# Four-layer graph network, layer 3: a wait for landed gathers in front of every second gather group

## What is computed

```python
def step(xk, _):
    msg = norm[:, None] * xk[src]
    agg = jax.ops.segment_sum(msg, dst, num_segments=n_nodes)
    return ((1.0 - ALPHA) * agg + ALPHA * h, None)
xK, _ = jax.lax.scan(step, x, None, length=10)
out = jax.nn.relu(xK)
```

## Time and profile before

| | us |
|---|---|
| median of the runs | 4953.56 |
| lowest and highest run | 4930.44, 4966.02 |
| span of the profiled execution | 6157.9 |
| of it layers 0, 1, 2 with what lies between | 3450 |
| of it layer 3, from its first gather | 2708 |

### The profile page before, as it was taken

How to read it: one execution, slowest core, us unless ns; L and a number is a source line. 1 busy time by engine, 2 the same in 40 slices (tenths; PEclk the granted TensorE clock), 3 DMA queues, 4 the chain that set the end, 5 groups by cost and what they waited for, 6 DMA issues and landing times.

```text
span 6157.9 us, 72323 instructions
## 1 busy us (share of the span) xinstructions
PE 4502.8 (73%) x25760; PEld 2814.8 (46%) x25760; DVE 2553.7 (41%) x8838; ACT 1022.9 (17%) x2922; POOL 3237.6 (53%) x3390
## 2 busy tenths in 40 slices
PE   3778477888775445446555788988888898888888
PEld 2556355566554334344444343434443444444344
DVE  6778444445443445555567422222222222222222
ACT  4656311111111000001222200000000000000001
POOL 3232365566555555555553365565656556565655
PEclk8888688899887666667767999989999999999999
DMA  5222222122222222222221555555555555555554
GB/s 136 77 83 79 77 56 52 51 58 59 55 55 57 67 70 75 68 68 69 65 71 42 160 173 159 171 158 164 172 167 164 166 178 166 161 174 161 165 170 135
DMA packets 455501, 686.46 MB, mean 111 GB/s; under 512 B 91793, under 2 KB 237879, under 8 KB 455120
## 3 DMA queue, kind: packets, MB, share of 16 engines
q1 hardware_dynamic: 341188, 454.71, 23.5%
q0 software_dynamic: 107584, 223.83, 14.0%
q10 hardware_dynamic: 6364, 3.20, 0.2%
HBM read 599.50 MB, written 82.31 MB: 111 GB/s over the span
## 4 chain that ended last, share of the span: by engine, by line
PE 42%; another core or an unknown queue 24%; DVE 18%; issue 11%; ACT 3%; DMA 1%; ACTq 0%; SPq 0%; DVEq 0%; POOL 0%; POOLq 0%
PE ps L2007 27%; PE ps L1751 5%; DVE E L2458 4%; DVE B L2538 2%; PE pt L2102 2%; DVE arena L2580 1%; PE ps L1828 1%; PE ps L2093 1%; PE pt L2038 1%; PE ps L2022 1%; DVE O L3023 1%; PE pt L1719 1%; ACT E L1561 1%; DVE scores L3019 1%
## 5 line engine op out<-in xcount | busy, mean ns | idle before, releaser
L2007 PE MATMUL ps<-arena,E 128*128 128x512 fp8e4 (+1 forms) x4900 | 1147.0, 385 | 93.6 <-issue 84.8
L2007 PE MATMUL ps<-arena,A 128*128 128x512 fp8e4 (+1 forms) x4900 | 1142.1, 385 | 62.4 <-issue 60.1
L1052 POOL DMA_INDIRECT arena<-table,src_i x810 | 776.9, 959 | 685.7 <-DMA table<-E 255.0
L1017 POOL DMA_INDIRECT E<-gat_table,src_i x782 | 759.3, 971 | 634.6 <-DVE arena L2580 367.7
L1052 POOL DMA_INDIRECT arena<-x_spill,src_i x810 | 775.3, 957 | 579.0 <-issue 225.8
L1002 POOL DMA_INDIRECT arena<-table,src_i x782 | 742.8, 950 | 583.5 <-issue 217.1
L1751 PE MATMUL ps<-E,arena 128*128 128x352 f32 (+22 forms) x2932 | 783.6, 421 | 241.1 <-DVE E L2458 155.4
L2007 PEld LDWEIGHTS ps<-arena,E 128*128 128x128 f16 x4900 | 471.4, 100 | 648.6 <-issue 193.9
L2007 PEld LDWEIGHTS ps<-arena,A 128*128 128x128 f16 x4900 | 472.9, 100 | 608.9 <-issue 154.8
L1751 PEld LDWEIGHTS ps<-E,arena 128*128 128x128 f32 x2932 | 515.4, 211 | 441.4 <-issue 195.5
L2909 DVE SCALAR_TENSOR_TENSOR C<-ps,sc_b,scores 128x128 f32<-128x128 f32 x490 | 138.9, 345 | 1295.1 <-PE ps L2022 769.3
(11 more groups left out here) (350 smaller groups left out, 4557.6 us busy)
## 6 DMA issues: line engine op xcount, KB each, us to landing
arena<-adj SPq DMA_DIRECT2D x180, 1024.0 KB
arena<-adj SPq DMA_DIRECT2D x90, 1088.0 KB
adj<-E SPq DMA_DIRECT2D x39, 784.0 KB
arena<-table,src_i POOLq DMA_INDIRECT x1592
O<-dst_rows SPq DMA_DIRECT2D x112, 224.0 KB
arena<-adj SPq DMA_DIRECT2D x20, 768.0 KB
x_spill<-A SPq DMA_DIRECT2D x55, 256.0 KB
arena<-x_spill,src_i POOLq DMA_INDIRECT x810
```

The source lines that it names most:

```text
L1017: pool.indirect_dma_start(out=att_rows[:, b % 3 * AB + at, :], out_offset=None, in_=gat_table, in_offset=bass.IndirectOffsetOnAxis(ap=src_ ...
L1052: pool.indirect_dma_start(out=y_rows[:, g % ERING, k, :], out_offset=None, in_=(table, x_spill)[half], in_offset=bass.IndirectOffsetOnAxis ...
L2007: mm = pe.matmul(chunk_banks[n % 2][:, 0:len(some) * P], y[:, i, h * D:(h + 1) * D], adj_ring[:, piece % ADJ_RING, 0:len(some), at:at + P] ...
```

## The change

In front of the gathers of groups g = 2, 4, ... 40 of each step, twenty times a step, GpSimd also waits on the `y_in` semaphore of group g - 1, the last group that it has issued, until all that group's gathers have landed. The ring, the plan and all other engines' instructions are as before.

```diff
                             for g in range(EGROUPS):
                                 pool.wait_ge(sem("edge_used"), pairs * (2 * EGROUPS) + (half * EGROUPS + g + 1))
                                 settle(pool)
+                                if g and g % 2 == 0:
+                                    r = (g - 1) % ERING
+                                    pool.wait_ge(y_in[r], (2 * pairs + half) * row_loads[r] + y_in_before[r]
+                                                 + 16 * sum(group_size(q) for q in range(r, g, ERING)))
                                 for k in range(group_size(g)):
                                     tile = edge_first + g * EG + k
                                     pool.indirect_dma_start(
```

## The result

| | us |
|---|---|
| before, median of 4 runs | 4959.79 |
| after, median of 4 runs (5393.62 to 5413.01) | 5409.67 |
| ratio, 95% interval | 1.0906 (1.0865 to 1.0947) |
| profiled execution of after, span | 5411.0 |
| profiled execution of before, seen ahead of the prediction | 6157.9 |

The forecast was 5170 with a range of 4935 to 5310. The sign came out as told, and so did the mechanism (waits of GpSimd that TensorE has to wait out). The loss is 450 us where 215 were forecast, outside the range, and also above the 375 us of the forecast's own outermost bound.

The account below looks back on a forecast made before the run. TensorE bounds layer 3 at 230 us a step; with the waits GpSimd's loop becomes 202.5 + 38 + 1.8 + 9.2 = 251.5, exposing 21.5 a step, 215 in ten: 4953.6 + 215 = 5169, rounded to 5170 us, range 4935 to 5310.

Parts of the forecast that it names:

- What bounds the kernel: Layer 3: TensorE sets the pace at 230 us a step; GpSimd is hidden with some 16 us to spare.
- The account of the median: Whole kernel: 4953.6 us can't hold both layer 3 at 2708 us and gathers of 1.25 us in layers 1 and 2.
- TensorE's own step: Layer 3: 220 us of matmuls and turns plus 9.3 us of waits for ScalarE, taken as 230 us a step.
- The price of a wait: GpSimd in layer 3: each added wait costs 1.9 us, bounds 1.5 to 2.2; twenty make 38 us a step.
- long-landings rival: Layer 3: gathers land later after an empty queue, adjacency pieces sharing the engines; 2.9 us a wait, 5370 us; chance 0.07.
- The last landing: End of GpSimd's loop in a layer 3 step: the last group's gathers take about 1.8 us to land.
- The forecast's 21.5: Layer 3: us exposed per step, GpSimd's loop after the change of 251.5 against TensorE's 230.
- group against group: Layer 3 check: GpSimd falls back 2.2 us per two groups, 44 a step, of which 34 are exposed.
- The profiled span: Profile of the changed kernel: 6160 to 6260 us, only 0 to 10 us a step longer, moving far less than the median.
- Hidden waits: Rival, layer 3: the added waits fall into GpSimd's rest; 4940 to 5000 us, most likely 4960; chance 0.29.
- Fewer transfers help TensorE: Rival, layer 3: an emptied gather queue relieves a third of TensorE's 248 us of "issue" stalls, 83 us, giving 4870; chance 0.07.
- The page's figure: A 64 KB GpSimd gather takes 2.15 us, so a wait adds 0.9 us, 18 us a step, costing next to nothing.

Follow-up runs that it names:

- e0: The kernel before, unchanged, profiled a second time: 4926.36 us in a single execution, profile span 4924.3 us.
- e8: The changed kernel, with SP loading 1/64 or less of each adjacency piece's bytes from layer 3's second step on: 5222.51 us, ratio 1.0537.
- e2: The changed kernel with the wait in front of every eighth group only, 5 waits a step instead of 20: 5045.09 us, ratio 1.0227.
- e1: The changed kernel with the wait in front of every fourth group only, 10 waits a step instead of 20: 5159.88 us, ratio 1.0450.
- e4: The changed kernel with the wait in front of every group, 40 waits a step instead of 20: 5835.29 us, ratio 1.1753.

## Why the prediction was wrong in its size

**What bounds the kernel: right.** TensorE set the pace, with GpSimd close behind, and layers 1 and 2 run at the gathers' 1.25 us. The account of the median, that the first profile's stalls and 1.25 us a gather can't both hold, came to the right side; e0 shows both halves of it.

**TensorE's own step: mis-sized by 10 us.** Its work was added up to 220 us, and 220.4 is what e0 measures in its usual step. Then I put 9.3 us of waits for ScalarE on top, from the earlier trace rows. e0 has 0.4 us of that wait in ten steps: it went with the stretch like the "issue" lines, only under another name. I had dropped the one and kept the other. Since TensorE's step is the cover under which waits are free, that error went into the forecast with its full size.

**The price of a wait: mis-sized, 1.9 us where 2.43 was measured** (2.73 idle in place of the 0.30 pause), above the upper bound of 2.2. Both rows are single gathers whose packets met little other traffic. The one of layer 2 had a DMA share of 0.16 beside it. The one of layer 3 was lucky in its moment: its packets ran between 3722 and 3723 us, when SP's queue took 0.02 of the DMA engines, against 0.85 in the microsecond before and 0.81 in the one behind. In after, the waits beside SP's packets run from 1.7 to 6.0 us; one row could not tell their mean. A wait "over 2.5 us", named ahead as a sign of being wrong, came true. e8 with its loads gone has 1.53 (1.83 - 0.30), near the lower of my bounds. The long-landings rival named the adjacency pieces, and gave 2.9 us and 5370: it was nearest to the result, at a chance of 0.07.

**The last landing: 4.1 us where I had 1.8**, from the end of the last gather to the end of its use. In e8 it is 2.7, so 1.4 of the 2.3 us went with the adjacency loads; the rest is the floor of a landing and the use itself, which I had left out.

**The sum again** with what was measured: 202.5 + 20 x 2.43 + 4.1 + 9.2 = 264.4 us, and 2.0 for gathers that are 1.2625 us apart on average instead of 1.25: 266.4, as measured. Less e0's mean of 221.3 that is 45.1 us a step, 451 in ten, where 450 were lost. Against the usual step of 220.4 it is 46. The forecast's 21.5 lacks 10.6 (the price), 9.6 (TensorE's step), 2.3 (the last landing) and 2.0 (the slower gathers). The other way that I worked it out, group against group, gave 34 us a step and stood only as a check: it had no wait for ScalarE in it, and so was nearer. Its price of a wait was the same 1.9, so part of its being near is luck. I should have asked why two sums of the same thing differ by 12 us.

**The profiled span: wrong.** I expected the profile of after at 6160 to 6260 us, since I took the stretch for something that a profile of this kernel has. It is 5411.0, and e0's is 4924.3; the sign "the profiled span moves far less than the median" failed with it. What stretched the first one isn't known; no run was made on it.

**The rivals.** Hidden waits: out, by e0 (no rest) and e2 (five waits cost 2.3%). Fewer transfers help TensorE: out; no dense matmul got shorter, and the "issue" idle that it was to relieve isn't there in either undisturbed profile. Its support was also misread: of the 21.3 us without idle time in the earlier trace rows, 16 ran beside gathers, which began at 4526.36.

**The page's figure.** The estimate from the Trainium skill, page "DMA: Bandwidth & Descriptors", section "Anatomy of one DMA — SWDGE (gpsimd) path", was 2.15 us from issue to landing for 64 KB. With hardly any other traffic e8 has 0.94 + 1.80 = 2.74 us from the start of a gather's record to the next gather behind the wait; the semaphore's own update comes 2.5 us after the record's start, and GpSimd goes on 0.26 us later. With the adjacency loads it is 3.67 us to the next gather on average. So the page's figure is some 0.4 us low for this gather alone, and 1.2 us low in after, where the update comes 3.4 us after the record's start on average.

**The signs named ahead.** POOL waits for its own gathers about 200 times after every eighth gather, the full-ring rest falls, line 2042 waits for gathered rows: seen. TensorE's waits do not stand in the later part of a step alone; from the fourth step on the first comes 40 to 60 us in. "The dense matmuls don't change in length" holds in part: those of 512 columns average 391 and 394 ns (two buffers) where e0 has 379 and 380, because of the stretches at the lower clock. The prediction had no term for that, and as said at e8 it cost nothing here.

## What to carry to other kernels

A wait for a landing costs the issuing engine the whole latency of one transfer, under the traffic that runs beside it at that moment, so price it in the stage where it will stand, and from many rows: here 1.8 us alone and 3.2 us beside SP's transfers. A wait one group further back, for gathers issued 5 us earlier, was free. When a profile is a quarter longer than the runs, drop all idle time of the stretched engine or none, work out its step from its work alone, and get a second number for the cover, because it is the cover that decides what is exposed.

## What the runs showed of the hardware that was not expected

- The landing of a 64 KB gather has a very narrow floor: 1.73 to 1.91 us idle from record's end to next gather in nine tenths of e8's waits; beside adjacency loads it reached 6.0 us (after).
- The same program was profiled at 6157.9 and at 4924.3 us. In the long one TensorE's idle time goes by "issue" and as waits for ScalarE, and GpSimd seems to rest 415 us in layer 3; in the short one there is no "issue" line, 0.4 us of the wait for ScalarE, and no pause of GpSimd for a full ring that is longer than the common 0.30 us.
- TensorE's granted clock falls to its lower level in short stretches once its work is broken up by waits: 3 stretches in layer 3 of e0 (16 us), 11 in e2 (45 us), 27 in e1 (109 us), 55 in after (256 us), 114 in e4 (463 us).
